# A two-layer adapter network on one core: two of SyncE's orders at the head of the second layer are changed

## The chip, the core and the metric

One core of a Trainium2 chip runs the whole program. The metric is the device time of one launch in microseconds. The kernel before took 2011.21 us, the median of 3 runs (2009.75 to 2011.28).

## What is computed

The input `x` has 128 batches of 64 channels by 1024 columns, 8192 rows of 1024 in all. Each of the two layers first conditions `x` by a matrix chosen per batch and then runs a 1024 x 1024 product, and adds the result to `x`:

```python
# layer 0: per-batch 64x64 mix, then a base product with 8 gated low-rank experts
c  = einsum('bct,bcd->bdt', x, weights[ids0])
x  = x + c @ W_base.T + b_base + sum over the top 2 of 8 experts (rank 16)
# layer 1: a base product with a LoRA adapter chosen per batch (32 adapters, rank 16)
r  = x @ base_weight.T + base_bias + (x @ A[ids1].T) @ B[ids1].T
q  = fp8(r / input_scale)
x  = x + (q @ fp8(weight / weight_scale)) * scales + bias
```

## The kernel before

The rows are cut into 64 tiles of 128 (two batches each). A first phase runs layer 0 over all tiles and writes each tile's result to two scratch tensors in DRAM: `x1_scratch` (plain, for the residual) and `x1t_scratch` (in turned 32 x 32 blocks, for the next product). A second phase runs layer 1 over all tiles. The float32 products are made exact by splitting each operand into a high and a low part, three products each. The change lies at the head of the second phase, in the instruction stream of SyncE, which issues every DMA.

The second phase, tile by tile, with the lines of the profile:

- SyncE `load_turned(t, b)` (line 452) brings the turned tile into `xbuf[b]`, a part of `ring`. ScalarE (line 688) makes `st_h` from it, in two halves, and VectorE (line 771) makes `st_l`. ScalarE then copies the previous tile's three result groups to `val` (line 705), so in its own order the next tile's halves stand ahead of these copies.
- SyncE `load_a` (line 464) brings an adapter's A part into `raw`; GpSimd `fill_slot` (line 598) copies it into the weights `w1h` and `w1l` and raises `slot_done`. SyncE `load_b` (line 471) brings three pieces of B into `b_stack[b]`.
- TensorE runs the main products (lines 1049 to 1051) in three groups g, each of which waits until `val` of the previous tile's same group is copied, because they share the PSUM banks. Before the first group it waits for `st_l` and for `slot_done`. Then come the LoRA products (line 1095) from `b_stack`, and then the second product of the previous tile, `ffn(t - 1)` (line 1062), which waits for `rqt_in`.
- VectorE rounds `val` to fp8 values in six steps (`quantize`, lines 879 to 897) and raises `rq_done`. SyncE then turns `rq` into `rqt` with one DMA transpose, `turn_rq` (line 510), which raises `rqt_in`.
- GpSimd adds the last bias (`bias_sb` in the rows, `bias2_sb` in the code, loaded at line 498) to the residual that `load_x1` (line 456) brought, into `obuf` (line 617), and raises `x1b_done`. VectorE adds `ffn`'s result (line 906, `finish`), and SyncE stores (line 504, `store_out`).

SyncE works strictly in the order written. At the head of the phase it issues: two rows of bias for both `b_stack`s; `load_turned(1, 1)`; the six B transfers of tile 0; two waits for the scratch stores; the last bias; `load_x1(1, 1)`. Then comes `tile(t, ...)` for each tile, whose steps are: the adapter loads for tile t + 1 (behind waits for `r_ps[2]` and `slot_done`, which say that the buffers are free); the turning transfer of tile t - 1's `rq`; the store of tile t - 2; and, behind a wait for `st_l` (`lo_done`) and one for `x1b_done`, `load_turned` and `load_x1` for tile t + 2 (the wait of line 533). Tile 0 is called with `first` true and has no turning transfer and no store; tile 1 has `first` and `lag` false, so no store; tiles 2 to 63 have `lag` true. The names with `_done`, `_in`, `_ps` and `_loaded` are semaphores.

Of the kernel before, what the change touches and what calls it, by code (L numbers as in the profile page):

```python
# [29 lines left out]
P = 128  # L30
# [3 lines left out]
KC = D // P  # L34
# [48 lines left out]
def build(nc, x, ids0, ids1, wc, m0, b0, b_base, w1t, base_bias, a1, b1, wf, bias2, s_in, s_w, out):  # L83
# [12 lines left out]
    with ExitStack() as whole:  # L96
        def sb(name, shape, dt, stack=whole):
            return stack.enter_context(nc.sbuf_tensor(name, shape, dt))

        def sem(name):  # L100
            return whole.enter_context(nc.semaphore(name))
# [34 lines left out]
        s_const = sem("s_const")  # L136
# [132 lines left out]
        with ExitStack() as p2:  # L269
# [10 lines left out]
            rqt = sb("rqt", [P, D], BF16, p2)  # L280
            bias2_sb = sb("bias2_sb", [P, D], F32, p2)
# [5 lines left out]
            bias2_loaded = sem("bias2_loaded")  # L287
# [16 lines left out]
            rq_done = sem("rq_done")  # L304
            rqt_in = sem("rqt_in")
# [39 lines left out]
        with nc.Block() as block:  # L345

            @block.sync
            def _(sp):
# [6 lines left out]
                def load_cond(t, r):  # L355

                    for j in range(PER_TILE):
                        which = sp.value_load(ids0_sb[0:1, bass.ds(PER_TILE * t + j, 1)], min_val=0, max_val=15)
                        rows = slice(j * CH, (j + 1) * CH)
                        sp.dma_start(wpair[rows, r, :],  # L360
                                     wc[bass.ds(which, 1)].rearrange("a c d -> (a c) d")).then_inc(wc_loaded[r], 16)
# [61 lines left out]
                def tile(t, r, more):  # L423

                    sp.wait_ge(x1_done[2], t + 1)
                    sp.dma_start(x1_dram[bass.ds(t, 1)].rearrange("a p n -> (a p) n"),
                                 ring[:, r, :]).then_inc(x1_stored, 16)

                    sp.wait_ge(blocks_done, t + 1)
                    to = x1t_dram[bass.ds(t, 1)].rearrange("o (q i) (a m) -> a (o i) q m", i=32, a=4)  # L430
                    for a in range(4):
                        sp.dma_start(to[a], x1_blocks[32 * a:32 * a + 32, :].rearrange("i (q m) -> i q m", q=4))\
                          .then_inc(blocks_stored, 16)
                    if more:

                        sp.wait_ge(x1_stored, 16 * (t + 1))
                        sp.dma_start(ring[:, r, :], x_t[bass.ds(t + RING, 1)].rearrange("a p n -> (a p) n"))\
                          .then_inc(x_loaded[r], 16)
                        load_cond(t + RING, r)

                for t in range(UNROLLED):
                    tile(t, t % RING, True)
                    feed(t)
                with sp.Fori(UNROLLED, TILES - 2 * RING + 1, RING) as i:
                    for r in range(RING):
                        tile(i + r, r, True)
# [4 lines left out]
                def load_turned(t, b):  # L451
                    sp.dma_start(xbuf[:, b, :], x1t_dram[bass.ds(t, 1)].rearrange("a p n -> (a p) n"))\
                      .then_inc(turned_loaded[b], 16)

                def load_x1(t, b):
                    sp.dma_start(x1buf[:, b, :], x1_dram[bass.ds(t, 1)].rearrange("a p n -> (a p) n"))\
                      .then_inc(x1_loaded[b], 16)

                def adapter(row, j):
                    return sp.value_load(ids1_sb[0:1, bass.ds(PER_TILE * row + j, 1)], min_val=0, max_val=LORAS - 1)  # L460

                def load_a(which, b, j):

                    sp.dma_start(a_raw[:, b, j, :], a1_dram[bass.ds(which, 1)].rearrange("a p c -> (a p) c"))\
                      .then_inc(a_loaded[b], 16)

                def load_b(which, b, j):

                    for s, part in enumerate((0, 0, 1)):
                        row = s * LR + j * RANK  # L470
                        sp.dma_start(b_stack[b][row:row + RANK, :].bitcast(F32),
                                     b1_ids[bass.ds(which, 1), :, part, :].rearrange("a r n -> (a r) n"))\
                          .then_inc(b_loaded[b], 16)
# [16 lines left out]

                for b in range(2):
                    sp.dma_start(b_stack[b][3 * LR:STACK, :].bitcast(F32), bias_dram).then_inc(bias_rows, 16)
                load_turned(1, 1)
                for j in range(PER_TILE):
                    load_b(adapter(0, j), 0, j)
                sp.wait_ge(x1_stored, 16 * TILES)
                sp.wait_ge(blocks_stored, 64 * TILES)
                sp.dma_start(bias2_sb[:, :], bias2.partition_broadcast(P)).then_inc(bias2_loaded, 16)
                load_x1(1, 1)

                def store_out(t, b):

                    sp.wait_ge(out_done[1], t + 1)
                    sp.dma_start(out_t[bass.ds(t, 1)].rearrange("a p n -> (a p) n"), obuf[:, b, :])\
                      .then_inc(out_stored[b], 16)

                def turn_rq(to, ks):

                    cols = slice(ks.start * P, ks.stop * P)
                    return sp.dma_start_transpose(to[:, cols].rearrange("p (k n) -> p k n", n=P), rq[:, cols])  # L510

                def tile(t, b, first, lag, more):
                    if more >= 1:
                        if not first:

                            sp.wait_ge(r_ps[2], t)
                            sp.wait_ge(slot_done, t)
                        for j in range(PER_TILE):
                            which = adapter(t + 1, j)
                            if not first:  # L520
                                load_a(which, 1 - b, j)
                            load_b(which, 1 - b, j)
                    if not first:

                        sp.wait_ge(s_const, 32)
                        sp.wait_ge(rq_done, t)
                        turn_rq(rqt, range(KC)).then_inc(rqt_in, 16)
                    if lag:
                        store_out(t - 2, b)
                    if more == 2:  # L530

                        sp.wait_ge(lo_done[1], TILES + t + 1)
                        sp.wait_ge(x1b_done, t + 1)
                        load_turned(t + 2, b)
                        load_x1(t + 2, b)
# [8 lines left out]
                for n, ks in enumerate(last_parts):  # L544
                    sp.wait_ge(rq_done, TILES + n)
                    turn_rq(rqt_last, ks).then_inc(rqt_last_in[n], 16)
# [6 lines left out]
            def _(pool):  # L553
# [10 lines left out]
                def split(n):  # L564

                    _, width, hi, lo, _ = pool_places(n)
                    piece = raw[:, n % 2, 0:width]
                    pool.wait_ge(pool_loaded[n % 2], 16 * (n // 2 + 1))
                    if n == tables:

                        pool.wait_ge(split_stored, 32 * tables)
                    pool.tensor_scalar(hi, piece, 1.0, None, ALU.mult).then_inc(pool_hi, 1)
                    pool.wait_ge(pool_hi, n + 1)
                    pool.tensor_tensor(lo, piece, hi, ALU.subtract).then_inc(pool_lo, 1)
# [54 lines left out]
            def _(act):  # L629
# [13 lines left out]
                for n, unit in enumerate(w0_units):  # L643
                    _, width, hi, _ = w0_places(unit)
                    act.wait_ge(stage_loaded[n % slots], 16 * (n // slots + 1))
                    act.activation(hi, stage[n % slots][:, 0:width], ACT.Copy,
                                   scale=LORA_SCALE if unit[0] == "b" else 1.0).then_inc(w0_hi, 1)
                    if n == 1:
                        st_hi(0, None)
# [69 lines left out]
            def _(dve):  # L719
# [29 lines left out]
                for n, unit in enumerate(w0_units):  # L749
                    _, width, hi, lo = w0_places(unit)  # L750
                    dve.wait_ge(w0_hi, n + 1)
                    piece = stage[n % slots][:, 0:width]
                    if unit[0] == "b":
                        dve.scalar_tensor_tensor(lo, piece, LORA_SCALE, hi, ALU.mult, ALU.subtract).then_inc(w0_lo, 1)
                    else:
                        dve.tensor_tensor(lo, piece, hi, ALU.subtract).then_inc(w0_lo, 1)
                    if n == 1:
                        for h in range(2):
                            turn_y(0, 0, pairs_to(0), h)
                            st_lo(0, h)  # L760
# [421 lines left out]
```

## Time and profile before

| | |
|---|---|
| median of 3 runs | 2011.21 us |
| the profiled execution, time | 2010.24 us |
| the profiled execution, span | 2008.1 us |
| mean granted TensorE clock | 0.996 |
| TensorE busy | 1973.0 us, 98% |
| VectorE busy | 1437.2 us, 72% |
| GpSimd busy | 494.7 us, 25% |
| ScalarE busy | 400.1 us, 20% |
| DMA | 144 GB/s in the mean |
| chain that ended last | TensorE 91%, VectorE 5% |

The profile comes from one execution. A timeline gives the start from the beginning of the span, the duration, the engine, the line, the operation and how many instructions were merged; in square brackets stands how long the engine had idled and what released it. The time of a transfer "to landing" counts from the start of its issue on SyncE to its semaphore. The granted clock is a share of full speed; TensorE's has two levels. All times below are of the second phase's head, which begins near 1007 us, if nothing else is said.

### The profile page before, as it was taken

How to read it: one execution, taken by the hardware profiler on the slowest of the kernel's cores; microseconds unless marked ns; L12 is line 12 of the kernel's file. 1: busy time of each engine (PE TensorE's matmuls, PEld its weight loads, DVE VectorE, ACT ScalarE, POOL GpSimd, SP SyncE). 2: the span in 40 equal slices, each digit the busy share in tenths (PEclk: the TensorE clock that was granted, in tenths of full speed). 3: DMA queues.
4: the chain of work that ended last, by engine and by line, in shares of the span. 5: the costliest groups of instructions: out<-in, count | busy, mean ns of one | idle time of the engine just before them, and what ended most of it. 6: DMA issues, size and time to landing. Idle time of an engine off the chain costs nothing.

```text
span 2008.1 us, 38332 instructions
## 1 busy us (share of the span) xinstructions
PE 1973.0 (98%) x13056; PEld 1809.6 (90%) x13056; DVE 1437.2 (72%) x3881; ACT 400.1 (20%) x1083; POOL 494.7 (25%) x471
## 2 busy tenths in 40 slices
PE   6999999999999999999999999999999999999998
PEld 5998999999999999999988888888888888888887
DVE  6888878778766666666667766776677667766776
ACT  3111211212211111111121222122212221212121
POOL 2444343210110110110122222222222222222222
PEclk9999999999999999999999999999999999999999
DMA  6765444334334334333356655665566656665663
GB/s 208 211 207 149 125 144 145 104 118 125 104 104 120 96 96 127 97 96 118 105 158 175 160 162 149 175 159 162 149 173 160 161 150 170 161 161 152 169 163 108
DMA packets 220523, 290.07 MB, mean 144 GB/s; under 512 B 98102, under 2 KB 169784, under 8 KB 220476
## 3 DMA queue, kind: packets, MB, share of 16 engines
q1 hardware_dynamic: 220476, 289.57, 51.6%
q8 instruction: 15, 0.25, 0.0%
q14 instruction: 32, 0.26, 0.0%
HBM read 163.63 MB, written 109.06 MB: 136 GB/s over the span
## 4 chain that ended last, share of the span: by engine, by line
PE 91%; DVE 5%; issue 1%; DMA 1%; SPq 1%; ACT 1%; POOL 0%; DVEq 0%; ACTq 0%; POOLq 0%
PE bank_g L990 12%; PE bank_g L992 12%; PE bank_g L991 12%; PE bank_g L1051 12%; PE bank_g L1050 12%; PE bank_g L1049 12%; PE bank_y L1062 11%; PE bank_y L970 3%; PE bank_g L1095 1%; PE bank_g L1019 1%; PE bank_g L1017 1%; PE bank_g L1018 1%; DVE hwt L327 1%; DVE wq_pow L785 0%; DVE x_blocks L860 0%
## 5 line engine op out<-in xcount | busy, mean ns | idle before, releaser
L990 PE MATMUL bank_g<-w0h,st_h 128*128 128x384 f32 (+1 forms) x1536 | 526.0, 342 | 10.3 <-DVE ring L849 5.4
L992 PE MATMUL bank_g<-w0h,st_l 128*128 128x384 f32 (+1 forms) x1536 | 520.7, 339 | 0.0
L991 PE MATMUL bank_g<-w0l,st_h 128*128 128x384 f32 (+1 forms) x1536 | 520.7, 339 | 0.0
L1049 PE MATMUL bank_g<-w1h,st_h 128*128 128x352 f32 x1536 | 505.2, 329 | 0.5 <-ACT val L705 0.5
L1051 PE MATMUL bank_g<-w1h,st_l 128*128 128x352 f32 x1536 | 496.0, 323 | 0.0
L1050 PE MATMUL bank_g<-w1l,st_h 128*128 128x352 f32 x1536 | 495.1, 322 | 0.0
L990 PEld LDWEIGHTS bank_g<-w0h,st_h 128*128 128x128 f32 x1536 | 289.2, 188 | 27.6 <-issue 20.3
L771 DVE TENSOR_TENSOR st_l<-ring,st_h 128x512 fp32r<-128x512 f32 x128 | 142.3, 1112 | 228.5 <-ACT st_h L688 228.4
L1049 PEld LDWEIGHTS bank_g<-w1h,st_h 128*128 128x128 f32 x1536 | 288.6, 188 | 8.1 <-issue 0.8
L562 POOL TENSOR_TENSOR ring<-ring,b_base_sb 128x1024 f32<-128x1024 f32 x64 | 152.8, 2402 | 564.3 <-PE bank_y L970 534.3
L1050 PEld LDWEIGHTS bank_g<-w1l,st_h 128*128 128x128 f32 x1536 | 288.5, 188 | 1.6
L991 PEld LDWEIGHTS bank_g<-w0l,st_h 128*128 128x128 f32 x1536 | 289.5, 188 | 0.0
L992 PEld LDWEIGHTS bank_g<-w0h,st_l 128*128 128x128 f32 x1536 | 289.2, 188 | 0.0
L1051 PEld LDWEIGHTS bank_g<-w1h,st_l 128*128 128x128 f32 x1536 | 288.9, 188 | 0.0
L1062 PE MATMUL bank_y<-wq,rqt 128*128 128x512 bf16 x1008 | 230.3, 382 | 2.3 <-DMA rqt<-rq 2.3
L617 POOL TENSOR_TENSOR obuf<-ring,bias_sb 128x1024 f32<-128x1024 f32 x64 | 154.9, 2420 | 181.7 <-DMA out<-obuf 172.8
L1062 PEld LDWEIGHTS bank_y<-wq,rqt 128*128 128x128 bf16 x1008 | 93.7, 98 | 116.3 <-DMA rqt<-rq 2.6
L598 POOL TENSOR_TENSOR w1h<-raw,ones 128x128 fp32r<-128x128 f32 x128 | 48.8, 402 | 575.6 <-DMA raw<-a_split 555.7
L327 DVE CAST hwt<-hw_parts 32x64 fp32r<-32x64 f32 x768 | 148.5, 193 | 11.8
L746 DVE TENSOR_TENSOR st_l<-bank_t,st_h 128x512 fp32r<-128x512 f32 x128 | 88.0, 687 | 91.2 <-ACT st_h L640 91.2
L688 ACT ACTIVATE st_h<-ring 128x512 fp32r<-128x512 f32 x128 | 80.9, 632 | 340.8 <-PE bank_g L1051 337.2
L640 ACT ACTIVATE st_h<-bank_t 128x512 fp32r<-128x512 f32 x128 | 76.7, 599 | 292.6 <-PE bank_g L992 168.9
(78 smaller groups left out, 1986.6 us busy)
## 6 DMA issues: line engine op xcount, KB each, us to landing
ring<-x SPq DMA_DIRECT2D x64, 512.0 KB, 3.9
x_scratch<-ring SPq DMA_DIRECT2D x64, 512.0 KB, 2.7
x1t_scratch<-x_blocks SPq DMA_DIRECT2D x256, 128.0 KB, 2.4
ring<-x1t_scratch SPq DMA_DIRECT2D x64, 512.0 KB, 3.6
ring<-x_scratch SPq DMA_DIRECT2D x64, 512.0 KB, 5.1
out<-obuf SPq DMA_DIRECT2D x64, 512.0 KB, 2.7
b_stack<-b_split SPq DMA_DIRECT2D x384, 64.0 KB, 3.7
raw<-a_split SPq DMA_DIRECT2D x128, 128.0 KB, 4.2
```

The costliest lines, as they stand in the source:

```text
L327: last = engine_move(hwt[32 * q:32 * q + 32, :, 32 * a:32 * a + 32], hw_parts[32 * a:32 * a + 32, :, 32 * q:32 * q + 32])
L562: pool.tensor_tensor(ring[:, r, :], ring[:, r, :], b_base_sb[:, :], ALU.add).then_inc(xb_done, 1)
L617: pool.tensor_tensor(obuf[:, b, :], x1buf[:, b, :], bias2_sb[:, :], ALU.add).then_inc(x1b_done, 1)
L746: dve.tensor_tensor(st_l[:, half], bank_t[:, :], st_h[:, half], ALU.subtract)\
L771: dve.tensor_tensor(turned(st_l[:, :], h), in_blocks(xbuf[:, b, :], h), turned(st_h[:, :], h), ALU.subtract).then_inc(lo_done[h], 1)
L990: pe.matmul(to, st_h[:, rows], w0h[:, k, cols], start=(k == 0), stop=False)
L991: pe.matmul(to, st_h[:, rows], w0l[:, k, cols], start=False, stop=False)
L992: last = pe.matmul(to, st_l[:, rows], w0h[:, k, cols], start=False, stop=(k == KC - 1))
L1049: pe.matmul(to, st_h[:, rows], w1h_k[:, k, cols], start=(k == 0), stop=False)
L1050: pe.matmul(to, st_h[:, rows], w1l_k[:, k, cols], start=False, stop=False)
L1051: last = pe.matmul(to, st_l[:, rows], w1h_k[:, k, cols], start=False, stop=(k == KC - 1))
L1062: last = pe.matmul(bank_f[:, h, :], rqt[:, k * P:(k + 1) * P], wq[:, k, h * HALF:(h + 1) * HALF], start=(k == 0), stop=(k == KC - 1))
```

## The change

Two places in SyncE's stream. In the head, the six B transfers of tile 0 now come ahead of `load_turned(1, 1)`, and the last bias is asked for right behind it and ahead of the two waits and `load_x1(1, 1)`. In `tile`, the turning transfer with its two waits becomes a function, `turn_tile`. For tile 1 alone (`not first and not lag`) it runs at the start, ahead of the waits and the adapter loads; for tiles 2 to 63 it runs where it did. No transfer is added or taken away, and no other engine's stream changes.

```diff
                 for b in range(2):
                     sp.dma_start(b_stack[b][3 * LR:STACK, :].bitcast(F32), bias_dram).then_inc(bias_rows, 16)
-                load_turned(1, 1)
                 for j in range(PER_TILE):
                     load_b(adapter(0, j), 0, j)
+                load_turned(1, 1)
+                sp.dma_start(bias2_sb[:, :], bias2.partition_broadcast(P)).then_inc(bias2_loaded, 16)
                 sp.wait_ge(x1_stored, 16 * TILES)
                 sp.wait_ge(blocks_stored, 64 * TILES)
-                sp.dma_start(bias2_sb[:, :], bias2.partition_broadcast(P)).then_inc(bias2_loaded, 16)
                 load_x1(1, 1)
...
+                def turn_tile(t):
+
+                    sp.wait_ge(s_const, 32)
+                    sp.wait_ge(rq_done, t)
+                    turn_rq(rqt, range(KC)).then_inc(rqt_in, 16)
+
...
                 def tile(t, b, first, lag, more):
+                    if not first and not lag:
+                        turn_tile(t)
                     if more >= 1:
...
-                    if not first:
-
-                        sp.wait_ge(s_const, 32)
-                        sp.wait_ge(rq_done, t)
-                        turn_rq(rqt, range(KC)).then_inc(rqt_in, 16)
+                    if lag:
+                        turn_tile(t)
                     if lag:
                         store_out(t - 2, b)
```

## Rows read from the trace of the kernel before

**Rows 1.** Timeline of TensorE: start, us, line, tile, xcount [idle before <-releaser]

```profile
1019.82 0.40 PE L1049 MATMUL bank_g<-w1h,st_h 128*128 128x352 f32 x1 [0.51 <-ACT val L705]
...
1034.35 5.31 PE L1062 MATMUL bank_y<-wq,rqt 128*128 128x512 bf16 x16 [2.29 <-DMA rqt<-rq]
```

**Rows 2.** Busy time by stretch; PEclk, DMA share and GB/s stand last

```profile
1019.82:1032.06 12.24, 12.24 (x75) 11.95 (x75) 10.13 (x21) 2.50 (x7) 2.80 (x1) 1.00 0.74 218
...
1034.35:1039.32 4.97, 4.97 (x17) 1.93 (x17) 4.87 (x4) 0.00 (x0) 3.16 (x2) 0.66 0.11 26
1039.32:1051.50 12.18, 12.18 (x78) 12.03 (x76) 6.08 (x19) 1.59 (x5) 2.35 (x5) 1.00 0.75 195
201.60:205.10 3.50, 3.24 (x10) 2.79 (x11) 2.45 (x5) 1.40 (x3) 0.00 (x0) 0.51 0.00 0
```

**Rows 3.** Timeline of TensorE, a stall in layer 1

```profile
201.66 0.51 PE L1017 MATMUL bank_g<-b0h,hwt 128*128 128x256 f32 x1 [2.13 <-DVE hwt L327]
```

**Rows 4.** Timeline of SyncE's DMA issues

```profile
1011.93 0.36 SPq L452 DMA_DIRECT2D ring<-x1t_scratch  x1
1013.23 3.32 SPq L471 DMA_DIRECT2D b_stack<-b_split  x6
1016.65 0.37 SPq L498 DMA_DIRECT2D bias_sb<-bias  x1
...
1024.76 0.85 SPq L456 DMA_DIRECT2D ring<-x_scratch  x1
...
1028.95 0.35 SPq L464 DMA_DIRECT2D raw<-a_split  x1
...
1031.15 1.36 SPq L510 DMA_TRANSPOSE rqt<-rq  x1
1037.59 0.38 SPq L452 DMA_DIRECT2D ring<-x1t_scratch  x1
...
1044.07 1.25 SPq L510 DMA_TRANSPOSE rqt<-rq  x1
```

**Rows 5.** Timeline of VectorE

```profile
1020.60 0.69 DVE L879 TENSOR_SCALAR power<-val 128x1024 uint32<-128x1024 uint32 x1 [0.62 <-ACT val L705]
...
1022.06 3.30 DVE L884 TENSOR_TENSOR val<-val,power 128x1024 f32<-128x1024 f32 x1
...
1027.12 0.69 DVE L897 TENSOR_TENSOR rq<-rounded,nan_or 128x1024 bf16<-128x1024 bf16 x1
```

**Rows 6.** Landing of line 452's transfer issued at 1011.93

```profile
DMA to landing us min/median/max: 4.4/4.4/4.4
```

**Rows 7.** Timeline of ScalarE

```profile
1018.63 0.63 ACT L688 ACTIVATE st_h<-ring 128x512 fp32r<-128x512 f32 x1 [1.23 <-PE bank_g L1051]
1019.17 1.40 ACT L705 ACTIVATE val<-bank_g,inv_in 128x320 f32<-128x320 f32 x3
```

**Rows 8.** Timeline of GpSimd

```profile
1021.48 2.80 POOL L617 TENSOR_TENSOR obuf<-ring,bias_sb 128x1024 f32<-128x1024 f32 x1 [8.93 <-issue]
1032.79 0.81 POOL L598 TENSOR_TENSOR w1h<-raw,ones 128x128 fp32r<-128x128 f32 x2 [8.51 <-DMA raw<-a_split]
...
1034.72 2.79 POOL L617 TENSOR_TENSOR obuf<-ring,bias_sb 128x1024 f32<-128x1024 f32 x1
```

**Rows 9.** The page's part 6, DMA issues: xcount, KB each, median us to landing

```profile
ring<-x1t_scratch SPq DMA_DIRECT2D x64, 512.0 KB, 3.6
```

**Rows 10.** Line 884 over the whole span: min, median and max ns

```profile
L884 DVE TENSOR_TENSOR val<-val,power x65: 559/1226/3301, 1022.1 to 1998.4; 128x1024 f32<-128x1024 f32 x63, 128x640 f32<-128x640 f32 x1, 128x384 f32<-128x384 f32 x1
```

**Rows 11.** Landing of line 456's transfer issued at 1017.07

```profile
DMA to landing us min/median/max: 7.5/7.5/7.5
```

**Rows 12.** Landing of line 510's four transfers, 1020 to 1080

```profile
DMA to landing us min/median/max: 3.2/3.9/4.1
```

**Rows 13.** Timeline of SyncE's DMA issues, tile 3

```profile
1059.50 1.29 SPq L510 DMA_TRANSPOSE rqt<-rq  x1
```

**Rows 14.** Timeline of TensorE, tile 3

```profile
1066.97 3.63 PE L1062 MATMUL bank_y<-wq,rqt 128*128 128x512 bf16 x16
```

## The prediction

> **What bounds the kernel now.** I read the page first: TensorE is busy for 98% of the span and carries 91% of the chain that ended last, so an edit on SyncE is worth only the idle time of TensorE that it removes or makes. The view of who waited for whom shows that, in the whole second layer, TensorE idles for 0.51 us before tile 1, for 2.29 us before tile 0's second product (`ffn(0)`, in tile 1) [rows 1], and once more behind the last tile. The change stands around the first two.
>
> The 2.29 us costs more than itself. `ffn(0)` should start when tile 1's LoRA products end, at 1034.35 - 2.29 = 1032.06, and starts at 1034.35 [rows 1]. The stretch that follows takes 4.97 us at a mean granted clock of 0.66: 4.97 x 0.34 = 1.69 us lost at the lower of the two levels (1.2 instead of 2.4 GHz) [rows 2]. A stall of 2.13 us in layer 1 is also followed by the low level (3.50 us at 0.51, 1.7 us lost); the stall of 0.51 us is not (1.00) [rows 1, 2, 3]. So the price to be won is 2.29 + 1.69 = 3.98 us, and no more: nowhere else in this layer does the change meet a stall.
>
> Next I read SyncE's order. The turning transfer goes out at 1031.15 [rows 4], while `rq` is complete at 1027.12 + 0.69 = 1027.81 [rows 5]. For 3.3 us SyncE was busy with the adapter loads ahead of it. That speaks for the change. What TensorE's 0.51 us wait hides speaks against it, below.
>
> **Part 1: the order at the head of layer 2.** `load_turned(1, 1)` moves behind the six transfers of `load_b`. It was issued at 1011.93 and landed 4.4 us later, at 1016.33 [rows 4, 6]. ScalarE wanted it only a little later, so this was on time by less than half a us; its second half ran at 1018.63 [rows 7]. Now the six B transfers start 0.40 us earlier (its issue slot) and take 3.32 us, and the load goes out at about 1013.23 - 0.40 + 3.32 + 0.10 = 1016.25. The bias follows at 1016.65, where it was: its place in time does not move at all, since as many instructions stand ahead of it; it is only no longer behind the two waits, which held nothing up. So the bias edit alone is worth nothing.
>
> The landing of the moved load decides. Its own 4.4 us gives 1020.65; the bias, issued in the same spot, took 1021.48 - 1016.65 = 4.8 us [rows 4, 8], and the median of these turned loads is 3.6 [rows 9]. I keep 1019.9 to 1021.1 and take 1020.65, the load's own. ScalarE then makes both halves and the first `val` copy one after another: two steps of 0.54 us (its pitch from 1018.63 to 1019.17) and 0.65 us from that copy to TensorE's start at 1019.82 [rows 1, 7]. TensorE starts tile 1 at 1020.65 + 1.73 = 1022.4 instead of 1019.82: a new stall of 0.51 + 2.6 = 3.1 us (2.3 to 3.5). It is longer than both stalls that were followed by the low clock [rows 1, 3], so I add the low level; as some of it falls into the stall itself, 1.3 us of the 1.7. Tile 1's main and LoRA products, 12.24 us [rows 2], then end at 1022.4 + 12.24 + 1.3 = 1035.9, against 1032.06: +3.9 us.
>
> **Part 2: the turning transfer ahead of the adapter loads in tile 1.** When is `rq` ready now? ScalarE's third `val` copy ends at 1020.65 + 1.08 + 1.40 = 1023.1 (before 1019.17 + 1.40 = 1020.57), and two VectorE steps of 0.73 us put line 884 at 1024.6 [rows 5, 7]. Line 884 took 3.30 us, its median being 1.23 [rows 5, 10], because GpSimd's add ran from 1021.48 to 1024.28; it ended 1.08 us after that [rows 8]. The add waits for the bias, which now has a 512 KB load just ahead of it. Bounds for what that adds: nothing (the slots are the same), or the 1024.6 - 1021.4 = 3.2 us by which the 512 KB load issued right behind the bias landed after it [rows 8, 11]. I take 1.4 us, nearer to the low end, since the same bytes have to move in the same stretch, which was used to 0.74 [rows 2]. Then: add 1022.9 to 1025.7, line 884 ends at 1026.8, `rq` is complete 1027.81 - 1025.36 = 2.45 us later as before (1025.36 is line 884's end), at 1029.2 (1027.9 to 1030.9), and the transfer lands 3.2 to 4.1 us after [rows 12], by 1033.3, before TensorE asks at 1035.9. The stall of 2.29 us and the 1.69 us behind it go: -3.98 us. Parts 1 and 2 cancel to within 0.1 us.
>
> The Trainium skill bears on the bias term. Its page "DMA: Bandwidth & Descriptors", section "Queues, rings and completion order", says that each DMA engine consumes an issuing queue's descriptors in ring order. By that rule the bias can't land in its old time once the turned load stands ahead; no row of the kernel before shows this pair. By the rule the sum keeps some of the delay, without it `rq` would be ready 1.4 us sooner.
>
> **Part 3: what is pushed back.** The adapter loads now stand behind a wait for `rq_done`. Queued behind it on SyncE are two A loads, six B loads, `load_turned(3, 1)` and `load_x1(3, 1)`, and, in tile 2, the next adapter loads and the next turning transfer. Before, the second A load went out 1028.95 - 1025.61 = 3.34 us after SyncE was free (1024.76 + 0.85), landed 3.84 us later, GpSimd filled the slot in 1.93 us (1032.79 to 1034.72) and added in 2.8 us, and `load_turned(3, 1)` followed at 1037.59, the turning transfer at 1044.07, 6.48 us behind it [rows 4, 8]. Now SyncE is free at 1029.2 + 1.36 = 1030.6. The second A load goes out at 1033.9, lands at 1037.8, and the slot is full at 1039.7. TensorE ends `ffn(0)` at 1035.9 + 3.28 = 1039.2 (3.28 is 4.97 less the 1.69), so tile 2 starts at 1039.7: a wait of 0.5 us. GpSimd's add ends at 1042.5; the turning transfer goes out 1044.07 - 1037.51 = 6.56 us after that, as before, at 1049.1, and lands 3.6 us later (between its 3.2 and 4.1), at 1052.7. TensorE asks for it at 1039.7 + 12.2 = 1051.9, where it had it at once at 1039.32 + 12.18 = 1051.5 [rows 2]. So `ffn(1)` waits 0.8 us and starts at 1052.7 instead of 1051.5: **+1.2 us**. Tile 3's turning transfer went out at 1059.50 and landed by 1063.6, 3.4 us before TensorE asked at 1066.97 [rows 12, 13, 14]. SyncE reaches the store in tile 2 about 2 us later than before, which this cover takes, so nothing more is lost. The sum is +1.2 us on the profiled execution, whose time is 2010.24 (its span of 2008.1 and 2.1 around it): 2011.4. The median of the timed runs is 2011.21, 0.97 above; on it the time is **2012.4 us**.
>
> This sum hardly depends on the clock in part 1. If the level stays high there, TensorE is 1.3 us earlier at `ffn(0)`, and then waits for the slot at 1039.7 all the same. The chain by `rq`, A load, fill, add and next turn is what sets `ffn(1)`.
>
> A second rule of the Trainium skill, page "SBUF — State Buffer", section "SBUF: two separate sides", says that VectorE and GpSimd hold their common ports exclusively, for the whole instruction, whichever starts first. Before, GpSimd was first. In tile 2 the order may turn over (line 884 at about 1038.9, the add at 1039.7); by the rule the add would end 0.4 us later and the sum would be +1.6 us. No row of this stretch shows that order.
>
> **Bounds.** With every short end (turned load 1019.9, bias not delayed, adds of 2.4 us) `rq` is ready at 1027.9, the slot is full at 1038.3, and the next turn lands at about 1050.2 to 1050.5: `ffn(1)` starts 1.0 to 1.3 us earlier than before. With the long ends (`rq` 1030.9, the A load 0.9 us slower) it starts at about 1055.
>
> **The rivals.** (A) The forecast: the gain is real and is given back by the late turned tile and the late adapter chain, -0.3 to +2.1 us, 2010.9 to 2013.3; chance 0.60. (B) The chain runs at its short ends and 0.3 to 1.5 us stay won: 2009.7 to 2010.9; for it, that GpSimd may get its bias on time; chance 0.20. (C) Slower: the adapter chain is so late that `ffn(1)` stalls for 2.1 us or more, and the clock falls a second time. It decides from a landing at 1053.6. Price: 2.1 + 1.7 = 3.8 us at the least, up to 3.6 + 1.7 = 5.3 (a landing at 1055): 2015.0 to 2016.5. For it speaks that a stall of 2.13 us did cost that [rows 2, 3]; against it, that four estimates would have to err to one side; chance 0.14. (D) Faster: the late turned tile costs nothing and all 3.98 us arrive: 2007.2. It needs the moved load to land by about 1017, 0.8 us after issue, where it took 4.4 [rows 6]; or a gap that I misread; chance 0.06. That the change doesn't do what it says is a part of (A): if `rq` were late enough, the turn would go out no earlier than 1031.15, and TensorE, itself late, would not notice.
>
> **How the numbers follow.** A difference of this kernel can be told from none at about 0.2%, 4.0 us. Faster by more: only (D), and its 3.98 us lie on the bound, 0.03. Slower by more: about half of (C), 0.07. The rest, 0.90, is within. The range leaves out (D) and the far end of (C), and takes in the long and short ends with 0.7 us for the spread of a median (the runs spread over 1.5 us): 2009.2 to 2015.2.
>
> **What would show it.** Right: a new stall of TensorE of 2.3 to 3.5 us at the head of tile 1, released through ScalarE by the turned tile; the clock at its low level behind it; no stall at `ffn(0)`; the turning transfer issued at about 1029; a stall of up to 2 us at `ffn(1)`, released by the transfer; `ffn(1)` starting 1.2 us later than before. Wrong: tile 1 starting by 1020 with the load issued after 1016; `ffn(1)` starting over 1.5 us earlier than before; or a new wait anywhere past tile 3.

## The result and the profile after

The changed kernel takes 2016.26 us, the median of 7 runs (2012.26 to 2018.21), against 2009.80 us for the kernel before, measured beside it (7 runs, 2007.7 to 2011.98). The ratio is 1.0029, with a 95% interval of 1.0018 to 1.0041: slower, by about 5.8 us. The profiled execution took 2016.62 us. The change added five lines ahead of most of the code, so line 1049 is now 1054, 1062 is 1067, 510 is 516, 705 is 710, 598 is 603, 617 is 622 and 884 is 889; what is line 884 now was 879.

The page: its span, and lines of parts 4 and 5:

```profile
span 2014.6 us, 38269 instructions
...
PE 89%; DVE 6%; issue 2%; DMA 1%; SPq 1%; ACT 1%; POOL 1%; DVEq 0%; POOLq 0%; ACTq 0%
...
L1054 PE MATMUL bank_g<-w1h,st_h 128*128 128x352 f32 x1536 | 506.4, 330 | 5.2 <-ACT val L710 2.6
```

TensorE is busy for 98% of the span as before; its idle time in front of the second layer's first products has grown from 0.5 to 5.2 us. Layer 2's first main product starts at 1007.91 us; before, it was 1006.92. This 0.99 us comes out of layer 1, where nothing was changed: of the 6.5 us between the two spans (2014.6 and 2008.1) it is no effect. To keep it out, I compare the kernels by one stretch, from layer 2's first main product to the first one of tile 3. It was 1054.78 - 1006.92 = 47.86 us, and is 1061.15 - 1007.91 = 53.24 us: 5.38 us longer, which is the rest but for 0.1 us. Behind tile 3 TensorE waits only at the very end (1.9 us, before 1.8).

Who TensorE waited for from 1003 to 1070 us (total, times, longest), and the timeline of these places, which answers [rows 1]:

```profile
PE bank_g L1054 <- ACT val L710: 2.6, 1, 2.6
PE bank_g L1054 <- POOL w1l L603: 2.5, 1, 2.5
PE bank_y L1067 <- DMA rqt<-rq: 2.1, 1, 2.1
```

```profile
1022.83 0.63 PE L1054 MATMUL bank_g<-w1h,st_h 128*128 128x352 f32 x1 [2.63 <-ACT val L710]
...
1043.77 0.43 PE L1054 MATMUL bank_g<-w1h,st_h 128*128 128x352 f32 x1 [2.55 <-POOL w1l L603]
...
1058.10 3.40 PE L1067 MATMUL bank_y<-wq,rqt 128*128 128x512 bf16 x15 [2.07 <-DMA rqt<-rq]
1061.15 0.51 PE L1054 MATMUL bank_g<-w1h,st_h 128*128 128x352 f32 x1
```

The stall of 2.29 us at `ffn(0)` is gone: there is no wait on line 1067 until 1058.10, which is `ffn(1)`. Three longer ones stand in its place: at the head of tile 1 (2.63 instead of 0.51 us), at the head of tile 2 for the adapter slot (2.55 instead of none) and at `ffn(1)` for the next turning transfer (2.07 instead of none).

The windows that answer [rows 2] (length, busy times, then granted clock, DMA share and GB/s): tile 1's products, `ffn(0)`, tile 2's products:

```profile
1022.83:1037.75 14.92, 14.92 (x75) 14.75 (x77) 9.82 (x21) 2.49 (x7) 2.38 (x1) 0.80 0.59 164
1037.82:1041.10 3.28, 3.27 (x15) 1.37 (x14) 2.44 (x4) 1.44 (x4) 1.51 (x3) 1.00 0.19 50
1043.77:1056.00 12.23, 12.23 (x75) 11.96 (x75) 7.26 (x18) 1.73 (x5) 3.78 (x5) 1.00 0.75 151
```

Tile 1's products take 14.92 us at a mean clock of 0.80, against 12.24 at 1.00: 2.68 us longer at the low level. `ffn(0)` now takes 3.28 us at 1.00, against 4.97 at 0.66. The sum of the differences is 2.12 + 2.68 - 2.29 - 1.69 + 2.55 + 2.07 = +5.44, the 5.38 us of the stretch. This is bookkeeping: it says where the time shows, not that one stall less would have saved its length, since the next wait may only have grown by it.

SyncE's issues, to be read against [rows 4]:

```profile
1017.48 0.41 SPq L452 DMA_DIRECT2D ring<-x1t_scratch  x1
...
1030.50 1.37 SPq L516 DMA_TRANSPOSE rqt<-rq  x1
...
1036.10 0.36 SPq L464 DMA_DIRECT2D raw<-a_split  x1
...
1046.33 0.36 SPq L452 DMA_DIRECT2D ring<-x1t_scratch  x1
...
1052.78 1.29 SPq L516 DMA_TRANSPOSE rqt<-rq  x1
```

The turned load of tile 1 goes out at 1017.48 and the turning transfer at 1030.50. From its end, 1031.87, to the second A load at 1036.10 SyncE needs 4.23 us. VectorE and GpSimd, against [rows 5, 8]:

```profile
1023.60 2.38 DVE L884 TENSOR_SCALAR power<-val 128x1024 uint32<-128x1024 uint32 x1 [0.53 <-ACT val L710]
...
1029.73 0.69 DVE L902 TENSOR_TENSOR rq<-rounded,nan_or 128x1024 bf16<-128x1024 bf16 x1
...
1040.82 1.30 DVE L889 TENSOR_TENSOR val<-val,power 128x1024 f32<-128x1024 f32 x1
1042.16 1.30 DVE L891 TENSOR_TENSOR rounded<-val,power 128x1024 bf16<-128x1024 f32 x1
...
1044.21 2.60 DVE L902 TENSOR_TENSOR rq<-rounded,nan_or 128x1024 bf16<-128x1024 bf16 x1 [0.21 <-DVE nan_or L893]
```

```profile
1023.06 2.38 POOL L622 TENSOR_TENSOR obuf<-ring,bias_sb 128x1024 f32<-128x1024 f32 x1 [9.53 <-issue]
1039.59 1.45 POOL L603 TENSOR_TENSOR w1h<-raw,ones 128x128 fp32r<-128x128 f32 x2 [14.15 <-DMA raw<-a_split]
1041.00 2.71 POOL L603 TENSOR_TENSOR w1l<-raw,ones 128x128 fp32r<-128x128 f32 x2
1043.68 2.58 POOL L622 TENSOR_TENSOR obuf<-ring,bias_sb 128x1024 f32<-128x1024 f32 x1
```

The add at 1023.06 stretches one step of the first rounding (2.38 us instead of 0.69), as before it stretched another. The four operations of the slot fill, 1039.59 to 1043.71, take 4.12 us, where they took 1.93. They lie beside VectorE's second rounding and end at 1043.71, 0.25 us behind its step of line 891. That rounding's last step (line 902) takes 2.60 us beside the add at 1043.68. So the last step ends at 1046.81, 3.1 us behind the fill.

### The profile page after: what moved, and what is told of

It is laid out like the page before. It is cut to its first block, busy times and chain, and to the rows that moved or that the text cites. A ratio compares the mean times of both kernels' runs of the same rounds, so it can differ in the third digit from the quotient of the medians.

```text
span 2014.6 us, 38269 instructions
## 1 busy us (share of the span) xinstructions
PE 1970.7 (98%) x12993; PEld 1813.1 (90%) x13056; DVE 1440.8 (72%) x3881; ACT 399.6 (20%) x1083; POOL 496.8 (25%) x471
## 4 chain that ended last, share of the span: by engine, by line
PE 89%; DVE 6%; issue 2%; DMA 1%; SPq 1%; ACT 1%; POOL 1%; DVEq 0%; POOLq 0%; ACTq 0%
PE bank_g L995 12%; PE bank_g L997 12%; PE bank_g L996 12%; PE bank_g L1056 12%; PE bank_g L1055 12%; PE bank_g L1054 12%; PE bank_y L1067 10%; PE bank_y L975 3%; PE bank_g L1100 1%; PE bank_g L1024 1%; PE bank_g L1022 1%; PE bank_g L1023 1%; DVE hwt L327 1%; DVE x_blocks L865 0%; DVE wq_pow L790 0%
## 5 line engine op out<-in xcount | busy, mean ns | idle before, releaser
L1067 PE MATMUL bank_y<-wq,rqt 128*128 128x512 bf16 x945 | 214.2, 379 | 6.4 <-DMA rqt<-rq 2.1
```

Source lines behind the costliest of these rows:

```text
L1067: last = pe.matmul(bank_f[:, h, :], rqt[:, k * P:(k + 1) * P], wq[:, k, h * HALF:(h + 1) * HALF], start=(k == 0), stop=(k == KC - 1))
```

## The experiments

In all of them the stretch is the one named above, from one profiled execution each. It contains the low clock where that fell (in this table: before, changed, turn_only, turn_hoist, after_a_first and bias_first, 1.4 to 2.8 us each), and one kernel can show it in one execution and not in the next; so a difference of 2 or 3 us between two stretches needs the waits beside it. The three kernels with the rounding cut (short_quant, turn_short, hoist_short) ran once each and were not timed. All the others ran beside the kernel before (29 runs, median 2011.22, for head_only, turn_only and a_first; 35 runs, median 2010.25, for the other four).

| kernel | ratio and 95% interval | stretch, us | against 47.86 |
|---|---|---|---|
| changed kernel | 1.0029 (1.0018 to 1.0041) | 53.24 | +5.4 |
| head_only | 0.9998 (0.9988 to 1.0007) | 47.15 | -0.7 |
| turn_only | 1.0013 (1.0003 to 1.0022) | 50.48 | +2.6 |
| a_first | 0.9988 (0.9978 to 0.9998) | 44.43 | -3.4 |
| turn_hoist | 1.0014 (1.0002 to 1.0026) | 50.38 | +2.5 |
| after_a_first | 0.9998 (0.9989 to 1.0007) | 47.96 | +0.1 |
| bias_first | 0.9997 (0.9988 to 1.0006) | 46.66 | -1.2 |
| a_first_bias | 0.9994 (0.9984 to 1.0003) | 45.29 | -2.6 |

**head_only: the head of the change alone.** The edit is the first hunk of the change; `tile` is as before.

> The head of the change alone (B transfers of tile 0 and the last bias ahead, the turned load of tile 1 behind them); tile 1 keeps its old order. Theory 1 (the changed kernel lost its time in a chain of adapter load, slot fill, add and next turn, which part two made late): tile 1 starts about 2 us late and TensorE runs about 2.7 us longer at the low clock, but the stall of 2.29 us at the second product and the 1.69 us behind it go, because TensorE itself is late; the slot is full in time, tile 2 starts within 0.5 us of TensorE's asking, and the kernel is within 2 us of before (ratio 0.999 to 1.001). Theory 2 (the loss is the low clock behind the new stall at the head of tile 1): this kernel loses what the changed one lost, 4 to 6 us, ratio 1.002 to 1.003.

Median 2010.46 us, ratio 0.9998. TensorE's waits in the stretch:

```profile
PE bank_g L1049 <- ACT val L705: 2.5, 1, 2.5
PE bank_y L1062 <- DMA rqt<-rq: 1.2, 1, 1.2
```

The first line is the new stall at the head of tile 1, 2.5 us. The second is the old stall, 1.2 us long now. The slot and the next turn come in time. So the head alone costs nothing that can be measured, as theory 1 had it, and theory 2 falls: the late turned load is paid out of the stall behind it. In this profile the clock did not fall behind the 2.5 us. Its twelve executions fall into two groups, six from 2007.1 to 2010.1 us at a mean clock of 0.997 or 0.998 and six from 2010.8 to 2013.3 at 0.995. That fits a low level that comes behind such a stall in some executions and not in others; but only one of the twelve has a trace, so where the clock of the others fell is not shown.

**turn_only: the turning transfer alone.** The edit is the second part of the change; the head is as before.

> Only the turning transfer of tile 1 ahead of the adapter loads; the head keeps its old order. Theory 1: the stall at the second product goes, but the slot for tile 2 fills only at about 1039 to 1041 us, TensorE waits 3.5 to 6 us for it, the next turning transfer goes out at about 1049, and the kernel is 1 to 6 us slower than before, ratio 1.0005 to 1.003. Theory 2: without the new stall at the head of tile 1 there is no low clock, and the 4 us of the old stall are gained, ratio 0.998 to 0.999.

Median 2014.43 us, ratio 1.0013. TensorE's waits, the window from tile 2's start, and GpSimd's slot fill:

```profile
PE bank_g L1054 <- POOL w1l L603: 4.1, 1, 4.1
```

```profile
1040.69:1055.00 14.31, 14.31 (x76) 14.18 (x76) 4.42 (x16) 1.60 (x5) 4.16 (x6) 0.83 0.69 175
```

```profile
1037.62 1.75 POOL L603 TENSOR_TENSOR w1h<-raw,ones 128x128 fp32r<-128x128 f32 x2 [13.02 <-DMA raw<-a_split]
1039.34 1.30 POOL L603 TENSOR_TENSOR w1l<-raw,ones 128x128 fp32r<-128x128 f32 x2
```

There is no stall at `ffn(0)`, and 4.1 us of waiting for the slot in its place, with a clock of 0.83 behind it: 14.31 x 0.17 = 2.4 us more. This edit alone makes the kernel slower, by about 2.6 us, with an interval that just leaves out 1. Theory 1 holds, and theory 2, by which it should have won 4 us, falls.

**a_first: the A loads ahead of the turning transfer, the B transfers behind it.**

```diff
+                        if not first and not lag:
+                            whiches = [adapter(t + 1, j) for j in range(PER_TILE)]
+                            for j in range(PER_TILE):
+                                load_a(whiches[j], 1 - b, j)
+                            turn_tile(t)
+                            for j in range(PER_TILE):
+                                load_b(whiches[j], 1 - b, j)
+                        for j in range(PER_TILE if first or lag else 0):
```

> The head keeps its old order; in tile 1 the two A loads go out first, then the turning transfer, then the six B transfers. Theory 1: the turning transfer goes out at about 1028.3 us and lands 3.2 to 4.0 us later, so 0 to 0.5 us of the old stall of 2.29 us are left and the clock stays high; the A loads are as early as before or earlier, so the slot is full by 1034 us and no later wait takes its place. Gain 3.0 to 4.0 us, ratio 0.998 to 0.9985. Rival: the turning transfer shares the DMA engines with what stands around it and lands late, so that the stall keeps 1 us or more; or the add of GpSimd and the line 884 change places and shift another wait; then 0 to 1.5 us.

Median 2008.22 us, ratio 0.9988: about 2.4 us faster than before, an interval that just leaves out 1. SyncE's issues and TensorE's waits:

```profile
1030.89 0.87 SPq L464 DMA_DIRECT2D raw<-a_split  x2
1031.86 1.37 SPq L516 DMA_TRANSPOSE rqt<-rq  x1
1033.34 3.58 SPq L471 DMA_DIRECT2D b_stack<-b_split  x6
```

```profile
PE bank_y L1072 <- DMA rqt<-rq: 0.5, 1, 0.5
PE bank_g L1059 <- ACT val L715: 0.4, 1, 0.4
```

Only the two A loads stand in front of the turning transfer. It goes out 0.3 us behind `rq` (complete at 1031.55) and lands after 4.4 us, which leaves 0.54 us of the old stall; the slot comes in time. The stretch is 3.4 us shorter, inside what was expected; the ratio is a little short of it, with the expectation inside the interval. The trace is of one of its slower executions (2010.45 us): in it layer 2 starts 3.7 us later than before, in a part that the edit does not touch. This is the only version whose interval lies below 1. What the change wanted was right; it moved the turn ahead of two loads too many.

**after_a_first: the same, on the head of the changed kernel.**

> The head of the changed kernel, but in tile 1 the two A loads go ahead of the turning transfer and the B transfers behind it. The changed kernel lost more than its two parts alone sum to (1.0029 against 0.9998 and 1.0013). Theory 1 (all of it is the chain of A load, slot, add and next turn, started late twice over): with the A loads ahead of it the waits of 2.55 us for the slot and of 2.07 us for tile 1's turning transfer are both under 0.5 us, only the wait of about 2.6 us at the head of tile 1 stays, with or without a low clock behind it, and no stall at the second product; stretch from layer 2's first main product to tile 3's 45.5 to 48.6 us (47.9 before, 53.2 changed), ratio 0.999 to 1.0005. Rival (the head itself costs more than its run alone shows): ratio over 1.001.

Median 2010.71 us, ratio 0.9998. TensorE has one wait in the whole stretch:

```profile
PE bank_g L1059 <- ACT val L715: 3.1, 1, 3.1
```

Tile 1's products behind it:

```profile
1022.74:1036.38 13.64, 13.64 (x75) 13.51 (x76) 10.48 (x21) 2.34 (x7) 6.24 (x6) 0.87 0.64 177
```

With the A loads ahead, the waits for the slot and for tile 1's turn are both gone. The 3.15 us stall at the head of tile 1 stays and was followed by the low clock (13.64 us for tile 1's products; in short_quant, with the same head and the high level, 12.08). With the A loads in front, then, the new head costs 3.5 us of stretch, all that a_first won, 1.6 us of it the clock; behind the old order it cost nothing, because it stood in for a stall. The changed kernel's excess over the sum of its parts (1.0029 against 1.0011) does not come from the head by itself, as the rival had it.

**short_quant: why the fill took 4.1 us.** The changed kernel, with tile 1's rounding cut to 32 columns:

```diff
-                with dve.Fori(2, TILES - 3, 2) as i:
+                tile(2, 0, 2, True, slice(0, 32))
+                tile(3, 1, 2, True)
+                with dve.Fori(4, TILES - 3, 2) as i:
```

> The changed kernel, with VectorE's six rounding steps for tile 1 cut to the first 32 of 1024 columns (the rest of that tile's rounded values is left out, so the output of tile 1 is not the reference's). It asks why GpSimd's slot fill for tile 2 took 4.1 us in the changed kernel and 1.9 us before. Theory 1 (VectorE's operations with two inputs in SBUF, which now run at the same time, hold the ports that both engines share): the fill takes 1.5 to 1.9 us, and TensorE's wait of 2.55 us before tile 2 falls to about 0.3. Rival (the fill is slowed by something else, the transfers for instance): the fill stays at about 4 us and the wait at about 2.5.

```profile
1038.12 0.76 POOL L603 TENSOR_TENSOR w1h<-raw,ones 128x128 fp32r<-128x128 f32 x2 [13.12 <-DMA raw<-a_split]
1038.83 0.75 POOL L603 TENSOR_TENSOR w1l<-raw,ones 128x128 fp32r<-128x128 f32 x2
```

The fill takes 1.47 us from its first start to its last end. So it was stretched by VectorE's rounding, as the theory had it. TensorE's wait for the slot fell only from 2.55 to 1.5 us, not to 0.3. I had left out that TensorE came sooner: its clock did not fall behind the 2.60 us at the head of tile 1 in this execution, and tile 1's products took 12.1 us and not 14.9. It fell instead behind the 2.06 us at `ffn(1)`.

**turn_hoist: the adapter numbers read ahead of the turning transfer.** On turn_only:

```diff
                     if not first and not lag:
+                        whiches = [adapter(t + 1, j) for j in range(PER_TILE)]
                         turn_tile(t)
```

> As the kernel with only the turning transfer moved (turn_only), but SyncE reads the two adapter numbers ahead of the turning transfer instead of behind it. There, SyncE needed 4.09 us from the end of the transfer's issue to the second A load; here the two reads (about 1.2 us each) are out of that stretch. Theory 1 (the wait for the slot follows the second A load one for one): the second A load goes out about 2.1 us sooner behind the turning transfer, TensorE's wait of 4.11 us before tile 2 falls to about 2.0, and the stretch from layer 2's first main product to tile 3's falls from 50.5 to 48.4 us or less; ratio 1.000 to 1.0008. Rival (the slot is late for the fill on GpSimd or for the landing, not for the issue): the wait stays over 3 us, ratio 1.001 to 1.0015.

Median 2013.81 us, ratio 1.0014; the wait for the slot is 3.83 us. Theory 1 falls in this form. The second A load goes out 2.68 us behind the transfer's end and not 4.09, but the fill ends only 0.5 us sooner:

```profile
1029.27 1.37 SPq L516 DMA_TRANSPOSE rqt<-rq  x1
...
1033.32 0.35 SPq L464 DMA_DIRECT2D raw<-a_split  x1
```

```profile
1036.70 2.55 POOL L604 TENSOR_TENSOR w1h<-raw,ones 128x128 fp32r<-128x128 f32 x2 [11.76 <-DMA raw<-a_split]
1039.21 1.48 POOL L604 TENSOR_TENSOR w1l<-raw,ones 128x128 fp32r<-128x128 f32 x2
```

It begins at 1036.70, 1.4 us sooner from layer 2's start than in turn_only, and takes 3.99 us instead of 3.02. I formed a new theory: the fill cannot end before VectorE's rounding does, whenever the A load comes. In these two traces it ends 0.6 and 0.3 us behind the rounding. Two runs tested it.

**turn_short and hoist_short: both kernels with the rounding of tile 1 cut**, by the edit of short_quant.

> turn_only, with VectorE's six rounding steps for tile 1 cut to the first 32 of 1024 columns (the rest of that tile's rounded values is left out). With turn_hoist the A load went out 1.4 us sooner relative to layer 2's start, and the slot for tile 2 was full only 0.4 us sooner: the fill on GpSimd grew from 3.0 to 4.0 us. Theory (VectorE's rounding holds the shared ports, so the fill ends with the rounding, whenever the A load comes): here the fill takes 1.5 us instead of 3.0 and TensorE's wait for the slot falls from 4.11 to about 2.6. Rival (the fill grows for another reason): fill 3 us, wait 4.1.

> turn_hoist with the same cut (tile 1's rounded values left out but for 32 columns). Theory: with VectorE out of the way the wait for the slot follows the A load again one for one: fill 1.5 us instead of 4.0, TensorE's wait 1.2 us instead of 3.83, that is 1.4 us under turn_short. Rival: fill 4 us, wait 3.8; or no difference to turn_short, if the landing of the A load and not its issue decides.

TensorE at tile 2's start, first of turn_short, then of hoist_short:

```profile
1041.80 0.43 PE L1056 MATMUL bank_g<-w1h,st_h 128*128 128x352 f32 x1 [2.56 <-POOL w1l L603]
```

```profile
1037.44 0.43 PE L1057 MATMUL bank_g<-w1h,st_h 128*128 128x352 f32 x1 [1.39 <-POOL w1l L604]
```

With VectorE out of the way the fill is 1.5 us in both, and the waits are 2.56 and 1.39 us, 1.17 apart, where they had been 0.28 apart (4.11 and 3.83). Not all of the 1.17 is the slot: TensorE also asked 0.4 us later in hoist_short. Counted from layer 2's start, the fill starts 0.8 us sooner and ends 0.8 us sooner; beside the rounding it had started 1.4 us sooner and ended 0.5 us sooner. So the rounding does hold the fill back. That the fill is pinned to the rounding's end is too strong: in the changed kernel it ended 3.1 us before the last step, and 0.25 us behind the two long steps with two operands. Both kernels have a wait of 2.2 and 2.3 us at `ffn(1)` for a turning transfer that lands late; see the last section.

**bias_first: the last bias ahead of tile 0's B transfers**, in the kernel before.

```diff
                 load_turned(1, 1)
+                sp.dma_start(bias2_sb[:, :], bias2.partition_broadcast(P)).then_inc(bias2_loaded, 16)
                 for j in range(PER_TILE):
                     load_b(adapter(0, j), 0, j)
```

> The kernel before with one transfer moved: the last bias is asked for right behind the turned load of tile 1 and ahead of tile 0's B transfers, 4.3 us sooner than in both kernels. Theory (GpSimd's add then ends before VectorE rounds, and SyncE comes to tile 1's adapter loads sooner): the add runs from about 1017 to 1019.4 us, VectorE's stretched operation (2.4 to 3.3 us) is short again, the turning transfer goes out at about 1028.6 instead of 1031.2, and the stall of 2.29 us falls to 0.5 or less. It is paid by tile 0's B transfers, which land 0.5 to 1.9 us too late for the first LoRA products. Net gain 1.5 to 3.5 us, ratio 0.998 to 0.9993. Rival: the B transfers behind 1 MB of other loads cost as much as is won, ratio 0.9995 to 1.001.

Median 2010.36 us, ratio 0.9997: the rival's result. TensorE in the stretch:

```profile
1021.34 0.71 PE L1095 MATMUL bank_g<-b_stack,ht 98*128 98x320 f32 x3 [1.63 <-issue]
1022.43 0.63 PE L1049 MATMUL bank_g<-w1h,st_h 128*128 128x352 f32 x1 [0.39 <-ACT val L705]
```

The stall at `ffn(0)` is gone, and TensorE waits 1.63 us ahead of the first LoRA products instead; the low clock follows. The row names no transfer as the releaser. I put the wait down to the B transfers, which now stand behind two loads of 512 KB: they landed 3.0 to 4.0 us after their issue, before 2.2 to 3.0. By that reading, what the bias wins, the B transfers lose.

**a_first_bias: both edits.**

> Both: A loads ahead of the turning transfer in tile 1 (a_first, which took 0.9988 of the time before) and the last bias 4.3 us sooner. If the rest of a_first's waits (0.54 us at the second product) is all that is left to win, this is within 1 us of it on either side: 0.5 us won, 0.5 to 1.5 us lost at the first LoRA products. Ratio 0.998 to 0.9992.

Median 2010.00 us, ratio 0.9994. The last 0.54 us at `ffn(0)` is gone and 1.70 us stand ahead of the LoRA products: 0.9 us worse than a_first by the stretch, as expected; the ratio is 0.0002 above the expected range. Here the clock stayed high behind the 1.70 us.

## Where the prediction was right and where wrong

The forecast was +1.2 us, 2009.2 to 2015.2; the median is 2016.26, outside. The forecast had the sign and the place of every wait. The step that failed is part 3, the time at which the slot is full and the next turn lands: `ffn(1)` started 5.6 us later than before and not 1.2. The clock term of part 1 was too small too. The times below are the changed kernel's less 0.99, so that they stand beside the prediction's.

**Part 1, the turned load.** Right in place, short in price. Issue at 1016.5 (said 1016.25), landing 3.6 us later, tile 1's start at 1021.8 (said 1022.4), a stall of 2.63 us (said 3.1):

```profile
1021.12 1.15 ACT L693 ACTIVATE st_h<-ring 128x512 fp32r<-128x512 f32 x2 [7.16 <-DMA ring<-x1t_scratch]
```

ScalarE makes both halves in one go, released by the turned load. That the bias edit alone is worth nothing was not tried by itself; the bias went out at 1016.95 where it was 1016.65, so its slot hardly moved. The clock term was 1.3 us and measured 2.68. I priced it from stalls whose low stretch was about 3.5 us long; here it lasted 5.9 us, to about 1027.7. In head_only and in short_quant stalls of 2.5 and 2.6 us were not followed by it at all. The term should have had both ends, 0 and 2.7.

**Part 2, the turn.** Right in the result, in part by luck: `rq` complete at 1029.4 (said 1029.2), the transfer issued at 1029.5, no stall at `ffn(0)` and no low clock behind. The add came at 1022.1 (said 1022.9), so the delay of the bias was 0.6 and not 1.4 us, and the rounding began 0.5 us sooner than I had it. Both should have made `rq` early. But the add now met the first step of the rounding and not the third, and the two errors cancelled. Of the 0.6 us, 0.3 is the later issue and 0.3 the landing, 5.0 us after issue instead of 4.7. The rule of the Trainium skill that the prediction named ("DMA: Bandwidth & Descriptors", "Queues, rings and completion order"), by which a queue's descriptors are taken in ring order, has the direction of this; at 0.3 us the trace agrees with it and proves no more.

**Part 3, what is pushed back.** Here the sum failed. Slot full at 1042.7 where I said 1039.7, of which

- 1.2 us is the second A load, 1035.1 instead of 1033.9: SyncE needed 4.23 us where I took 3.34 from before, and the transfer had gone out 0.3 us later;
- 2.2 us is the fill, 4.12 instead of 1.93 us, less 0.4 us for a quicker landing.

I had taken the fill's length from an execution in which only its end touched VectorE's rounding. Moving it 4 to 8 us put it beside the two steps with two operands in SBUF. I did cite the rule that bears on this, of the Trainium skill's page "SBUF — State Buffer", section "SBUF: two separate sides" (the two engines hold their common ports exclusively, for a whole instruction), but applied it to the add alone and at a price of 0.4 us. turn_short and hoist_short show what it is worth on the fill: 1.5 us alone, 3.0 and 4.0 beside the rounding. The trace agrees with the rule in that the fill's operations stretch beside the rounding (4.12 us instead of 1.5) and a step of the rounding stretches beside the add (2.60 us instead of 0.69). Beside the fill the rounding's steps grew by 0.07 us each.

From there the chain ran as told: turn issued 9.1 us behind the full slot (said 9.4), at 1051.8 instead of 1049.1, landing after 5.0 us where I took 3.6, another 1.4 us whose cause stays open (last section):

```profile
DMA to landing us min/median/max: 5.0/5.0/5.0
```

`ffn(1)` stalls 2.07 us and starts at 1057.1; I had said 1052.7, and 0.8 us.

**The bounds and rival C.** My long end for `ffn(1)` was 1055, with the fill at 1.93 us in it. Its bound should have been the fill beside the rounding. Rival (C), a chain so late that `ffn(1)` stalls for about 2 us, at 2015.0 to 2016.5, is the case that came, for part of its reason: the landing was past 1053.6, but what made it late were the slot and the transfer's own 5.0 us, `ffn(1)` waited 2.07 us and not 2.1 or more, and the clock did not fall a second time. I gave it 0.14.

That the sum "hardly depends on the clock in part 1" is neither upheld nor refuted. For it speaks that TensorE asked for the slot at 1040.2 and still waited 2.55 us; had it come sooner, it would have waited longer for the same slot. Against it, tile 1's rounding starts when TensorE ends tile 1, and the fill met that rounding, which the sum left out. turn_only, whose tile 1 ran at the high level, shows how much that can be. Less its own start (0.87 us later than before), its slot was full at 1039.8, 2.95 us sooner than in the changed kernel. Of this 1.59 us is the second A load, which went out at 1033.5 because `rq` was complete at 1028.0 and not at 1029.4; that is the late turned load and not the clock. 0.26 us is the landing, and 1.10 us the fill, 3.02 against 4.12. Only the last can come from the clock, and it was not tried by itself.

The excess of the changed kernel over its two parts is read from the same two traces. Its stretch is 2.76 us longer than turn_only's: tile 2 starts 2.96 us later, `ffn(1)` stalls 2.07 us where it did not, and tile 2's products are 2.08 us shorter, because the clock did not fall behind the slot. The clock also counts in the median. Of the changed kernel's seven executions, two with a mean clock of 0.997 took 2012.3 and 2013.6 us, inside the forecast's range, and five with 0.994 or 0.995 took 2016.1 to 2018.2. Only one of them has a trace, so where the others lost it is not shown.

## What to carry to other kernels

When a transfer is moved ahead of others on an in-order queue, ask of each one it passes who is next to need it, and re-time that consumer in its new place: a length read from the trace holds only beside the neighbours it had there. Split the group that is passed. Here two of eight transfers were urgent; left in front, they took 0.87 us of issues, most of it before `rq` was complete; put behind, they cost a stall longer than the one removed. And a stall in front of TensorE can have a second price, the clock: stalls of the same length here were followed by it in one trace and not in another, so carry it as a range from nothing.

## What the runs showed of the hardware

- VectorE and GpSimd stretch each other: the fill took 1.5 us alone and 4.12 us beside VectorE's rounding; beside GpSimd's add, a two-input add on VectorE took 3.30 us (kernel before) against 1.23 alone, and a single-input step 2.38 us (changed) against 0.69.
- The length of a stall alone does not tell whether the clock falls. It fell behind 2.29 us (before), 2.63 us (changed), 3.15 us (after_a_first), 3.83 and 4.11 us (turn_hoist, turn_only), behind 2.06 us (short_quant, `ffn(1)`: 4.96 us at 0.66), and behind 1.63 and 0.39 us close together (bias_first). It did not behind 2.52 us (head_only), 2.60 us (short_quant), 2.55 and 2.07 us (changed), 2.56 and 2.23 us (turn_short), 2.33 us (hoist_short), nor behind 1.70 and 0.39 us close together (a_first_bias). What decides between these was not tried.
- From the end of a turning transfer's issue to the second A load SyncE needed 4.1 to 4.2 us in four kernels, and 2.6 to 2.7 with the two adapter numbers read ahead of it. From the end of the plain load that stands there otherwise it was 3.3 to 3.4 us in tile 1, but 3.7 in tile 2 of the kernel before. Whether the transfer lengthens the reads stays open.
- Tile 2's turning transfer (of tile 1's `rq`) landed after 5.0 to 5.5 us in the changed kernel, short_quant, turn_short and hoist_short, and after 3.1 to 3.9 us in the kernel before and in the seven others. In those four the output store of 512 KB went out 1.55 us behind it, with no wait between them; in the others 1.8 us or more. But tile 3's in the changed kernel had its store 1.5 us behind it and landed after 4.1 us. Whether the store is the cause stays open.
